# Preparation of a next layer spread over more slots, and a capped mixture of experts with Silu on ScalarE and its down product in three parts

## The reference

```python
x = x + linear_attention(layernorm(x))
x = x + biased_ffn(layernorm(x))        # 8 experts, 2 chosen, and a shared one
x = x + wide_attention(layernorm(x))    # 16 heads of 64
x = x + biased_ffn(layernorm(x))        # same weights as before
x = x + rotary_attention(layernorm(x))  # 16 heads of 8, causal
x = x + capped_ffn(layernorm(x))        # 32 experts, 4 chosen, and a shared one
x = x + state_space(layernorm(x))       # scan over 256 positions, 128 x 64 states
x = x + capped_ffn(layernorm(x))        # same weights as before
```

```python
def _silu_and_mul(gu):
    g, u = jnp.split(gu, 2, axis=-1)
    return jax.nn.silu(g) * u
gu = jnp.einsum('ech,ehi->eci', buf[:, :C], w_gate_up)
expert_out = jnp.einsum('eci,eih->ech', _silu_and_mul(gu), w_down)
shared = _silu_and_mul(x @ shared_w_gate_up) @ shared_w_down
return (routed + shared).reshape(b, s, h)
```

## Time and profile before

| what | value |
|---|---|
| median of 3 runs | 1993.4 us (1988.6 to 1994.98) |
| the profiled execution: its time | 1988.01 us |
| its span, first to last instruction | 1986.2 us |
| TensorE (PE) busy | 1786.8 us, 90% |
| VectorE (DVE) busy | 1511.3 us, 76% |
| ScalarE (ACT) busy | 874.8 us, 44% |
| GpSimd (POOL) busy | 703.6 us, 35% |
| mean granted TensorE clock | 0.966 of full speed |
| DMA | 19.94 MB, mean 10 GB/s |

### The profile page before, as it was taken

The page is one execution under the profiler, slowest core; times in us unless marked ns, Lnnn a source line. Parts: engine busy times, 40 slices in busy tenths (PEclk is TensorE's granted clock), DMA queues, the critical chain, the costliest instruction groups (busy, mean ns, idle before and its releaser), DMA issues. The chain is left out here.

```text
span 1986.2 us, 23692 instructions
## 1 busy us (share of the span) xinstructions
PE 1786.8 (90%) x7574; PEld 932.4 (47%) x7581; DVE 1511.3 (76%) x2501; ACT 874.8 (44%) x2063; POOL 703.6 (35%) x802
## 2 busy tenths in 40 slices
PE   7879999999998999989998999888888888789999
PEld 2346654555554555546665555432222323225555
DVE  5868865555555588657767888699999999997887
ACT  3345544654545454345653333444354443333332
POOL 4722222333333222322220000077678686660000
PEclk9989999999999999979998999899999999999999
DMA  6000000000000000010000000000000000000000
GB/s 244 1 1 0 1 0 1 1 1 1 1 1 1 0 1 1 0 43 2 1 2 1 1 0 1 17 0 13 5 0 17 0 15 2 0 0 1 0 6 16
DMA packets 9787, 19.94 MB, mean 10 GB/s; under 512 B 1088, under 2 KB 8384, under 8 KB 8768
## 3 DMA queue, kind: packets, MB, share of 16 engines
q1 hardware_dynamic: 9664, 18.42, 2.7%
HBM read 14.22 MB, written 1.05 MB: 8 GB/s over the span
## 5 line engine op out<-in xcount | busy, mean ns | idle before, releaser
L2078 POOL TENSOR_TENSOR ssm_hc<-ssm_h,ssm_cm 128x512 f32<-128x512 f32 x256 | 334.6, 1309 | 155.2 <-DVE ssm_h L2122 154.9
L2122 DVE TENSOR_TENSOR_SCAN ssm_h<-banks,ssm_dbx 128x512 f32<-128x512 f32 x256 | 310.6, 1214 | 2.3 <-DVE ssm_dbx L2114 2.3
L307 PE MATMUL banks<-ffn_x_high,up_high 128*128 128x512 f32 x544 | 283.5, 521 | 13.9 <-ACT ffn_s1g L856 9.6
L2024 PE MATMUL banks<-ssm_hc,const 128*128 128x512 f32 x512 | 272.9, 615 | 12.2 <-DVE ssm_gated L2099 9.3
L2062 ACT ACTIVATE banks<-banks,a_neg 128x510 f32<-128x510 f32 x256 | 167.1, 659 | 248.0 <-PE banks L2011 247.1
L308 PE MATMUL banks<-ffn_x_low,up_high 128*128 128x512 f32 x544 | 216.9, 399 | 0.0
L309 PE MATMUL banks<-ffn_x_high,up_low 128*128 128x512 f32 x544 | 216.5, 398 | 0.0
L1498 POOL TENSOR_SCALAR wide_pin<-wide_pin,wide_rden 128x256 f32<-128x256 f32 x256 | 117.6, 478 | 226.1 <-DVE wide_rden L1516 226.1
L2114 DVE TENSOR_TENSOR ssm_dbx<-banks,ssm_bm 128x512 f32<-128x512 f32 x256 | 171.9, 672 | 13.5 <-PE banks L2014 11.4
L343 POOL TENSOR_TENSOR x_norm<-x_centred,x_square 128x512 f32<-128x512 f32 x32 | 41.3, 1291 | 395.1 <-ACT x_square L338 395.1
L1731 ACT ACTIVATE ffn_th<-banks 128x512 f32<-128x512 f32 (+1 forms) x136 | 81.1, 597 | 212.4 <-PE banks L309 190.2
(11 more groups left out here) (230 smaller groups left out, 3373.6 us busy)
## 6 DMA issues: line engine op xcount, KB each, us to landing
ssm_packed<-ssm_parts SPq DMA_DIRECT2D x48, 64.0 KB, 2.0
up_whole<-in_up SPq DMA_DIRECT2D x1, 2304.0 KB, 15.1
weights<-in_weights SPq DMA_DIRECT2D x1, 2048.0 KB, 22.4
up_whole<-in_up SPq DMA_DIRECT2D x1, 2048.0 KB, 8.5
half<-in_half SPq DMA_DIRECT2D x1, 1440.0 KB, 17.8
weights<-in_weights SPq DMA_DIRECT2D x1, 1168.0 KB, 24.7
weights<-in_weights SPq DMA_DIRECT2D x1, 1152.0 KB, 8.1
const<-in_const SPq DMA_DIRECT2D x1, 1042.0 KB, 10.0
```

The lines of the kernel that those rows point to most:

```text
L307: pe.matmul(out, w_high, x_high, start=True, stop=False)
L2024: pe.matmul(k.bank[5][:], k.c("hot")[:, P - row:2 * P - row], hc[:, i % HOLD, :], start=(i % NP == 0), stop=(i % NP == NP - 1)).then_inc(s ...
L2078: pool.tensor_tensor(hc[:, i % HOLD, :], h[:, i % HOLD, :], cm[:, i // NP % 2, :], ALU.mult) \
L2122: dve.tensor_tensor_scan(h[:, n % HOLD, :], k.bank[DELTA[n % AHEAD]][:], dbx[:, n % AHEAD, :], 0.0, ALU.mult, ALU.add).then_inc(s["h"], 1)
```

## The change

1. **Down product in parts.** The 16 down weights `d0` to `d15` move to the second up table (2 to 3 MB, twelve blocks to be cut, three to a pass of rotary attention). ScalarE rounds `a` to `a_high`, GpSimd subtracts it from `a` for `a_low`, and three products follow, of high weights with `a_high`, low weights with `a_high` and high weights with `a_low`. The step 0 product stays float32. The down product lags by four steps (`LAG`), the ring of `a` has eight places (`RING`).
2. **Silu on ScalarE** in place of Tanh, with VectorE's first product gone, and 1.0 for 0.5 in the selector. Silu's table set is not the one with Exp, so a switch to `natural_log_exp_and_others` is added ahead of the routing's Exp (n == 6).
3. **GpSimd's program** of the capped stage is now a loop over steps, with its preparation or guests in the slot before each subtraction.
4. **Slots.** The routing's last part is split in two (the split of the weights and the copy of the rows apart); `biased_ffn` in wide attention, rotary attention in `biased_ffn` and in its own passes, and the capped stage in rotary attention take other slots; rotary attention's ScalarE and GpSimd norm pieces come one slot later and `rot_km` is issued two and two.
5. **State space:** SyncE packs part by part, each as soon as it is split; `a_neg` is computed in guest pieces 0 and 12; two Tanh are in pieces of their own, and the table loads stand elsewhere.

```diff
-            layout([(f"{w}{p}", P) for p in range(E1 // 2) for w in ("g", "u")])]
+            layout([(f"{w}{p}", P) for p in range(E1 // 2) for w in ("g", "u")] + [(f"d{p}", P) for p in range(E1 // 2)])]
...
+    if n == 5:
...
-    if n == 5:
+    if n == 6:
...
-    return Stage(s, home, N, {"lin": (1, 2, 3, 4, 5, 6, 7, 9), "wide": (0,) * 7 + (1, 3, 3, 3, 4, 4, 5, 7, 8)},
+    return Stage(s, home, N, {"lin": (1, 2, 3, 4, 5, 6, 7, 9), "wide": (0,) * 7 + (1, 3, 3, 4, 5, 6, 7, 7, 8)},
...
+        for c in {14: (0, 1), 15: (2, 3)}.get(n, ()):
+            if c == 0:
+                pool.wait_ge(s["k"], p + 1)
+            pool.tensor_scalar(km[:, p % 2, c, :], kk[:], k.c("rows")[:, c:c + 1], 1.0, ALU.mult, ALU.mult) \
+                .then_inc(s["km"], 1)
...
-                for i in (2 * p, 2 * p + 1):
+                for i in range(3 * p, 3 * p + 3):
...
-    return Stage(s, home, NS, {"ffn0": (7, 8, 9, 10, 11, 12, 13, 14, 16)}, tensor, scalar, gpsimd, vector, run)
+    return Stage(s, home, NS, {"ffn0": (7, 8, 10, 11, 12, 13, 14, 15, 16)}, tensor, scalar, gpsimd, vector, run)
...
-                    if at_slot in (7, 8, 13):
+                    if at_slot in (7, 8, 11):
...
-    RING, LAG = 5, 2
+    RING, LAG = 8, 4
...
+            k.table(act, "natural_log_exp_and_others")
...
+                c = routed(g)
+                high, low = k.up_parts(1, f"d{n - 1}")
+                pe.wait_ge(s["a_high"], c + 1)
+                pe.matmul(k.bank[5][:], high, a_high[:, c % LAG, :], start=False, stop=False)
+                pe.matmul(k.bank[5][:], low, a_high[:, c % LAG, :], start=False, stop=False)
+                pe.wait_ge(s["a_low"], c + 1)
+                pe.matmul(k.bank[5][:], high, a_low[:, c % LAG, :], start=False, stop=(n == N - 1)) \
+                    .then_inc(s["down"], 1)
...
+            def cut_a(g):
+
+                if g % N == 0:
+                    return
+                c = routed(g)
+                act.wait_ge(s["act"], c + 1)
+                if c >= LAG:
+                    act.wait_ge(s["down"], step(c - LAG) + 1)
+                act.activation(a_high[:, c % LAG, :], a[:, g % RING, :], ACT.Copy).then_inc(s["a_high"], 1)
 
             for g in range(ALL):
                 rows, i = rows_of(g % N), g % 2
                 act.wait_ge(s["g"], g + 1)
                 if g >= 2:
-                    act.wait_ge(s["g_read"], g - 1)
-                act.activation(th[0:rows, i, :], k.bank[i][0:rows, :], ACT.Tanh, scale=0.5).then_inc(s["tanh"], 1)
+                    act.wait_ge(s["u_read"], g - 1)
+                act.activation(sg[0:rows, i, :], k.bank[i][0:rows, :], ACT.Silu).then_inc(s["silu"], 1)
+                if g >= 5:
+                    cut_a(g - 5)
...
+            for g in range(ALL - 5, ALL):
+                cut_a(g)
...
-            for p in range(1, PASSES):
-                prepare_gpsimd(k, pool, s, p)
+            for g in range(ALL):
+                c = routed(g)
+                if g // N + 1 < PASSES:
+                    gpsimd(pool, g // N + 1, g % N + 2)
+                else:
+                    follow.slot(g % N)
+                if g % N:
+                    pool.wait_ge(s["a_high"], c + 1)
+                    if c >= LAG:
+                        pool.wait_ge(s["down"], step(c - LAG) + 1)
+                    pool.tensor_tensor(a_low[:, c % LAG, :], a[:, g % RING, :], a_high[:, c % LAG, :].bitcast(F32),
+                                       ALU.subtract).then_inc(s["a_low"], 1)
...
-                i, o = g % 2, p1[:, g % RING, :]
-                dve.wait_ge(s["tanh"], g + 1)
-                dve.scalar_tensor_tensor(o[rows], th[rows, i, :], 1.0, k.bank[i][rows, :], ALU.add, ALU.mult) \
-                    .then_inc(s["g_read"], 1)
-                dve.wait_ge(s["g_read"], g + 1)
+                i = g % 2
+                dve.wait_ge(s["silu"], g + 1)
                 dve.wait_ge(s["u"], g + 1)
-                dve.tensor_tensor(o[rows], o[rows], k.bank[2 + i][rows, :], ALU.mult).then_inc(s["u_read"], 1)
+                if g >= RING:
+                    dve.wait_ge(s["down"], g - RING + 1)
+                    if (g - RING) % N:
+                        dve.wait_ge(s["a_low"], routed(g - RING) + 1)
+                ins = dve.tensor_tensor(a[rows, g % RING, :], sg[rows, i, :], k.bank[2 + i][rows, :], ALU.mult)
+                ins.then_inc(s["u_read"], 1)
...
-    return Stage(s, home, N, {"rot": (0,) * 6 + (1, 3, 5, 7, 8, 10, 11, 12, 14, 17),
+    return Stage(s, home, N, {"rot": (0,) * 6 + (1, 3, 5, 7, 8, 10, 11, 12, 13, 17),
...
+        for part in range(3):
+            sp.wait_ge(s["split"], 6 * p + 2 * part + 2)
+            for g in range(4):
```

98 lines of the change are left out of this document (48 added, 50 removed).

## The result

| | before | changed |
|---|---|---|
| median of 15 runs each | 1988.6 us (1986.3 to 1996.1) | 1994.9 us (1992.7 to 2004.7) |
| the profiled execution | 1988.01 us | 1994.62 us |
| its span | 1986.2 us | 1992.8 us |

The ratio is 1.004, with a 95% interval of 1.0026 to 1.0053: the change makes the kernel slower by 0.4%. The forecast was 1968, with a range of 1950 to 1988. Seven of the changed kernel's 15 runs took 2000.1 to 2004.7 us at a mean granted clock of 0.961 to 0.963, the other eight, the profiled one among them, 1992.7 to 1994.9 at 0.966 to 0.969, so the longer ones are in no trace here.

A forecast was written before the change was run, and what follows sets the result against it. TensorE was taken to bound the capped stages' own passes. Capped stages -7.6, guest slots -5, -6.5 and -4, rotary attention +0.5 gave -22.6: from 1988.0 to 1965.4, plus 2.7 for the median, 1968 us; range 1950 to 1988.

The forecast's parts named there:

- Part 1: Capped stages' down product: three products for one float32 product save 0.16 us a step, 20.9 over eight passes.
- rival 4: Down step: waits for `a_high` and `a_low` expose two weight loads of 0.19 a step, 2017 us; chance 0.07.
- Part 2: Capped stages: the other engines keep up with TensorE and lateness stays hidden; six own passes gain 15.6 us.
- The failing step: Own capped passes: VectorE 29.1, ScalarE 28.5, GpSimd 21.6 us stay under TensorE's 44.0; late Silu hidden by 3.1 to 3.35.
- The step on the split: Routing weights' split in its own slot: TensorE's wait of 0.9 unchanged, 0 a pass, bounds -0.9 to +0.9.
- Part 3: First capped stage's last pass: guest norm queued among GpSimd's subtractions, TensorE waits 3.5 to 6; +8 us, bounds 0 to +12.
- Part 4: Guests in other slots, in wide attention, second biased stage and rotary attention: -5, -6.5, -4 and +0.5 us.
- (a): Wide attention's last pass: cutting VectorE's routing burst removes the 4.75 wait for `wide_pt`; -5 us, bounds 0 to -9.
- (b): Second biased stage's last pass: ScalarE's 3.52 stop for the norm's product and low clock go; -6.5 us, bounds -3 to -8.
- (c): Second biased stage's last pass: `rot_km` behind the clamp saves 2.8 of ScalarE's 8.51 wait; -4 us, bounds -1 to -9.
- Rival 3: Capped stage: a table switch costs more than its load, making ScalarE's visits too late; 25 us, 1993; chance 0.05.
- rival 1: Guest slots don't pay: moved waits return a slot later, leaving (c)'s 2.8 and the capped stages' gain; 1981 us; chance 0.14.

The follow-up runs named there:

- Experiment 3: Kernel before, with 96 unused GpSimd subtractions added, one a routed step in the capped stages' own passes: 1998.3 us, ratio 1.0047.
- experiment 5: Changed kernel without the 128 GpSimd subtractions for `a_low`; the third product takes `a_high` again (different result): 1965.0 us, ratio 0.9875.
- Experiment 9: Changed kernel with Tanh for Silu and no table switch before the routing's exponential, two loads a pass fewer (wrong result): 1977.3 us, ratio 0.9949.
- experiment 4: Changed kernel with the capped stage of before put back, its routing parts in the new slots: 1992.9 us, ratio 1.0015.
- Experiment 8: Changed kernel with the capped stage of before in the new slots, split's turn and row copy one slot later: 1965.7 us, ratio 0.9879.
- experiment 6: Changed kernel with the residual addition first in its slot, and the split's turn and row copy one slot later: 1976.0 us, ratio 0.9932.
- experiment 2: Changed kernel with VectorE's residual addition in the capped stage issued first in its slot: 1984.0 us, ratio 0.9986.
- experiment 11: Experiment 6's kernel with the subtractions of the first capped stage's last pass on VectorE: 1969.9 us, ratio 0.9914.
- experiment 12: Experiment 8's kernel with the state-space function of before the change: 1974.5 us, ratio 0.9935.

## Why the prediction was wrong

In the two traces the kernel moved by +6.6 us and not by -22.6. Of the 29.2 between them 23.6 lie in the capped stages (+16.0 for -7.6), 7.1 in wide attention, the second biased stage and rotary attention (-7.9 for -15), and -1.5 in the two rows of the table that were put at 0.

**Part 1, right.** Three products for one, 0.23 apart: a step without waits of 2.32 to 2.34, forecast 2.33. No weight load of rival 4 shows in it.

**Part 2, where it failed.** Its durations were right (Silu 0.60, `a_high` 0.62, a load 1.28, a subtraction 1.29, TensorE 44.3 busy). The failing step is "Each is under TensorE's 44.0 ... hidden, narrowly": each lateness was held against the cover by itself, with VectorE's operations at their old length, and TensorE was to wait for nothing new. It waits 5.9 us in an own pass for 1.3 before.

- VectorE's operations were priced from a trace in which GpSimd was nearly idle (1.26 us a pass). Experiment 3 shows the price of the neighbour, 10 us, with nothing else of the change, and experiment 5 that the changed kernel is 30 us shorter without the subtractions. The Trainium skill, "SBUF — State Buffer", section "Who interferes with whom", says that a VectorE instruction with two SBUF inputs contends with a GpSimd instruction that reads SBUF for a pair of ports under an exclusive lock, and that casts and tensor_scalar can contend too. The traces agree (0.29 to 1.33, the cast 0.23 to 1.17). The sentence on GpSimd's 21.6 us should have carried a second half: whom it shuts out.
- The two loads around the exponential were found hidden at 1.8 late. Without subtractions they are (experiment 5, no wait for `ffn_a`); `r_exp`, which they delay as well, is what the routing's burst on VectorE starts from. Experiment 9 shows 17.6 us for them beside the subtractions.
- The step on the split ("Its bounds are -0.9 ... and +0.9") rested on its operations being the same. Their distance to the reader was not. In the changed kernel the wait is 0.8 in three own passes and 1.9 in three, 2.6 us more than before in all, so this term was small there and hardly out of its bounds. It is 2.9 in experiment 4, beyond the bound, with a clock of 0.79 on the mean behind it. The 27 and 8 us of experiments 8 and 6 are what a better slot gives; they are not what the change lost.
- The residual's move to slot 3 was in no term. The lag was counted as cover for the down product, and what else hangs on it (`residual` at `LAG - 1`) was not followed: 6.6 us of waits in the trace, 11 us by experiment 2.

**Part 3, half right.** The wait for the guest's norm was forecast as 3.5 to 6 and is 4.7. The stage cost more than the sum, though: experiments 6 and 8 differ by 18 us in it, most of it in its last pass. The queue made TensorE wait 4.7 for `a_low` as well, which no term had (experiment 11 takes most of such waits away). A part of the change put at nothing gave 8 to 9 back in the same place in experiment 12's comparison; if it does so in the changed kernel, two errors of opposite sign met there.

**Part 4, right in kind, too large.** (a) TensorE's long wait for `wide_pt` fell from 4.75 to 2.0, but the low clock only moved: the windows behind it, in the changed kernel, and at the end of the second biased stage:

```profile
648.00:656.00 8.00, 5.92 (x14) 2.60 (x14) 1.29 (x2) 0.60 (x1) 0.00 (x0) 0.50 0.00 0
836.00:860.00 24.00, 18.56 (x62) 8.36 (x63) 9.11 (x14) 6.64 (x23) 8.29 (x9) 0.55 0.32 127
```

so -1.2 for -5, which is within the scatter. (b) ScalarE's stop of 3.52 is gone, with the clock's fall from 812 to 820. (c) The wait for the clamp fell from 8.51 to 5.70, as forecast (2.8), but ScalarE's three waits for it from 790 to 860 sum to 12.9 for 13.8, since the next one grew from 0.56 to 2.44, and the clock stayed low all the same. Together (b) and (c) gave -6.1 for -10.5. Of the slots as a whole the sum was 15 us. Experiment 8 shows 23, with the split's turn later and the new state-space function, and experiment 12, without that function, 14. That is near the 15, but partly by luck: some 4 of it lie in the capped stages, where the sum had nothing for the slots, and 5 in wide attention, where twice the same code differed by 2.

**Rivals.** None of them was it. Rival 3 came near: it named the same two switches and a cost of 25 us, but by way of a longer load. The loads are as short as the rows said, and without two of them a pass the kernel is 17.6 us shorter (experiment 9). Of rival 1 something came as well: in (a) and (c) the low clock was found again a little further on. No one of the four gave the cost of a busy GpSimd or of the residual's new slot, so the range left out the result.
